# Keeping layer 0's residual in the PSUM bank of its aggregation (two graph layers, 16 graphs)

## The reference

```
def layernorm(x): m = mean(x, -1); v = var(x, -1); return (x - m) / sqrt(v + 1e-5)

# layer 0: scores between all pairs of nodes, masked by the adjacency
e0    = leaky(einsum('id,jd->ij', h * a0, h))         # slope 0.2
alpha = sigmoid(where(adj == 1, e0, -inf))
x     = layernorm(x + einsum('ij,jd->id', alpha, h) + bias)

# layer 1: attention from two projected vectors
Hh    = x @ W;  s = Hh @ a_src;  d = Hh @ a_dst
e     = where(adj != 0, exp(-leaky(s_i + d_j)), 0)
x     = layernorm(x + elu((e @ Hh) / rowsum(e)))
```

## Time and profile before

| | us |
|---|---|
| median of 3 runs | 1370.85 (1370.57 to 1371.18) |
| the profiled execution | 1369.6 |
| its span, first to last instruction | 1367.8 |

### The profile page before, as it was taken

The page is one execution under the profiler, slowest core; times in us unless marked ns, Lnnn a source line. Parts: engine busy times, 40 slices in busy tenths (PEclk is TensorE's granted clock), DMA queues, the critical chain, the costliest instruction groups (busy, mean ns, idle before and its releaser), DMA issues.

```text
span 1367.8 us, 27395 instructions
## 1 busy us (share of the span) xinstructions
PE 1275.9 (93%) x7874; PEld 1139.3 (83%) x7874; DVE 1029.2 (75%) x2594; ACT 856.0 (63%) x2130; POOL 842.4 (62%) x1228
## 2 busy tenths in 40 slices
PE   5799999999999999999999999999999998999986
PEld 4788888888888888888888888888888888888875
DVE  5777778787777877778777787877878777787865
ACT  4746757476575756757476575756757567574643
POOL 4746749476583855839466583865839567394732
PEclk9999999999999999999999999999999999999999
DMA  8162350614325162350624415153250623406001
GB/s 173 32 109 74 67 109 19 119 58 87 94 41 102 45 111 73 59 113 12 121 63 73 104 28 110 54 100 80 54 119 16 111 73 65 108 14 124 28 5 34
DMA packets 190352, 101.73 MB, mean 74 GB/s; under 512 B 140656, under 2 KB 173808, under 8 KB 190320
## 3 DMA queue, kind: packets, MB, share of 16 engines
q1 hardware_dynamic: 171888, 67.79, 21.2%
q0 software_dynamic: 18432, 33.56, 14.6%
HBM read 84.55 MB, written 16.78 MB: 74 GB/s over the span
## 4 chain that ended last, share of the span: by engine, by line
PE 39%; POOL 24%; DVE 20%; issue 11%; ACT 5%; DMA 0%; DVEq 0%; POOLq 0%; ACTq 0%
POOL coef_lo L369 13%; PE acc_bank L1227 11%; PE hh_bank L1206 5%; DVE coef L880 5%; PE acc_bank L1108 4%; PE acc_bank L1110 4%; PE acc_bank L1109 4%; PE lg_bank L1108 3%; PE lg_bank L1110 3%; PE lg_bank L1109 3%; POOL var_eps L377 3%; POOL rstd L380 2%; POOL rstd L390 2%; DVE stats L920 2%; DVE reluP L915 2%
## 5 line engine op out<-in xcount | busy, mean ns | idle before, releaser
L1227 PE MATMUL acc_bank<-H,coef 128*128 128x258 f32 x2048 | 469.1, 382 | 10.9 <-ACT reluP L606 9.6
L1227 PEld LDWEIGHTS acc_bank<-H,coef 128*128 128x128 f32 x2048 | 381.7, 190 | 73.7 <-issue 20.2
L369 POOL TENSOR_TENSOR coef_lo<-coef,coef_hi 128x1024 fp32r<-128x1024 f32 x128 | 305.7, 2389 | 62.2 <-ACT coef_hi L552 60.3
L1108 PE MATMUL acc_bank<-h_hi,coef_hi 128*128 128x256 f32 x1024 | 297.4, 290 | 0.0
L1110 PE MATMUL acc_bank<-h_hi,coef_lo 128*128 128x256 f32 x1024 | 286.3, 280 | 0.0
L1109 PE MATMUL acc_bank<-h_lo,coef_hi 128*128 128x256 f32 x1024 | 286.1, 279 | 0.0
L880 DVE SCALAR_TENSOR_TENSOR coef<-tr_bank,E_col,codeT 128x256 f32<-128x256 f32 x512 | 209.1, 476 | 39.3 <-PE acc_bank L1227 36.8
L1108 PEld LDWEIGHTS acc_bank<-h_hi,coef_hi 128*128 128x128 f32 x1024 | 194.8, 190 | 1.0
L1109 PEld LDWEIGHTS acc_bank<-h_lo,coef_hi 128*128 128x128 f32 x1024 | 195.0, 190 | 0.0
L1110 PEld LDWEIGHTS acc_bank<-h_hi,coef_lo 128*128 128x128 f32 x1024 | 194.7, 190 | 0.0
L552 ACT ACTIVATE coef_hi<-coef 128x1024 fp32r<-128x1024 f32 x128 | 135.7, 1060 | 84.6 <-DVE coef L819 84.1
(11 more groups left out here) (77 smaller groups left out, 2283.5 us busy)
## 6 DMA issues: line engine op xcount, KB each, us to landing
code_nat<-in_adj POOLq DMA_DIRECT2D x128, 256.0 KB, 5.3
x_raw<-in_x SPq DMA_DIRECT2D x16, 1024.0 KB, 5.6
out<-x SPq DMA_DIRECT2D x128, 128.0 KB, 1.7
codeT<-code_nat SPq DMA_TRANSPOSE x128, 3.3
W_ext<-in_L_gnn_W SPq DMA_DIRECT2D x1, 256.0 KB, 4.2
eluE<-in_L_gnn_a SPq DMA_DIRECT2D x1, 256.0 KB, 4.6
bias_bc<-in_L_gnn_bias SPq DMA_DIRECT2D x1, 128.0 KB, 4.1
a_col<-in_L_gnn_a SPq DMA_DIRECT2D x4, 1.0 KB, 4.6
```

The source lines that it names most:

```text
L369: nc.gpsimd.tensor_tensor(coef_lo[:, t % 4, :, :], blocks(coef[:, t % 4, :]), f32(coef_hi[:, t % 4, :, :]), ALU.subtract).then_inc(S.lo0, 1)
L1108: nc.tensor.matmul(dst, lhs_hi, rhs_hi, start=first, stop=False)
L1227: ins = nc.tensor.matmul(acc_bank[t % 2][:, 0:HC], coef[:, SLOT1[t], J * P:(J + 1) * P], H[:, J, :], start=J == 0, stop=J == NT - 1)
```

## The change

The SBUF tile `resid` goes. `residual0` writes its result over its own input, in columns 0 to 255 of the PSUM bank; `stats0` and `norm0` read it there. The bank is therefore free for the next matmuls only when `norm0` is done, so the two waits of PE that protected the bank change from the residual's semaphore to `x1`, with the same counts.

```
--- before.py
+++ after.py
@@ -192,7 +192,7 @@
         coef = sb("coef", [P, 6, N])
         coef_hi = sb("coef_hi", [P, 4, NT, P], FP32R)
         coef_lo = sb("coef_lo", [P, 4, NT, P], FP32R)
-        resid = sb("resid", [P, 2, D])
+
         stats = sb("stats", [P, 4, 6])
         moments = sb("moments", [P, 4, 2])
         var_eps = sb("var_eps", [P, 4, 1])
@@ -829,12 +829,12 @@
                 dve.wait_ge(S.agg0, NT * b + t + 1)
                 if t == 0:
                     dve.wait_ge(S.xb, NT * b + NT)
-                nc.vector.scalar_tensor_tensor(resid[:, t % 2, :], acc_bank[t % 2][:, 0:D], 0.5, xb[:, t, :],
+                nc.vector.scalar_tensor_tensor(acc_bank[t % 2][:, 0:D], acc_bank[t % 2][:, 0:D], 0.5, xb[:, t, :],
                                                ALU.mult, ALU.add).then_inc(S.resid0, 1)
 
             def stats0(S, b, t):
                 dve.wait_ge(S.resid0, NT * b + t + 1)
-                nc.vector.bn_stats(stats[:, t % 2, :], resid[:, t % 2, :]).then_inc(S.stats0, 1)
+                nc.vector.bn_stats(stats[:, t % 2, :], acc_bank[t % 2][:, 0:D]).then_inc(S.stats0, 1)
 
             def moments0(S, b, t):
                 dve.wait_ge(S.stats0, NT * b + t + 1)
@@ -846,7 +846,7 @@
                 if prev:
 
                     dve.wait_ge(S.out_stored[t], 16 * b)
-                nc.vector.tensor_scalar(x1[:, t, :], resid[:, t % 2, :], moments[:, t % 2, 0:1],
+                nc.vector.tensor_scalar(x1[:, t, :], acc_bank[t % 2][:, 0:D], moments[:, t % 2, 0:1],
                                         rstd[:, t % 2, :], ALU.subtract, ALU.mult).then_inc(S.x1, 1)
 
 
@@ -1167,7 +1167,7 @@
                     pe.wait_ge(S.h_lo, 4 * b + 4)
 
                 if t >= 2:
-                    pe.wait_ge(S.resid0, NT * b + t - 1)
+                    pe.wait_ge(S.x1, NT * b + t - 1)
                 elif prev:
                     pe.wait_ge(S.relu, NT * b + t - 1)
                 for J in range(NT):
@@ -1222,7 +1222,7 @@
                 if t >= 2:
                     pe.wait_ge(S.relu, NT * b + t - 1)
                 else:
-                    pe.wait_ge(S.resid0, NT * b + t + 7)
+                    pe.wait_ge(S.x1, NT * b + t + 7)
                 for J in range(NT):
                     ins = nc.tensor.matmul(acc_bank[t % 2][:, 0:HC], coef[:, SLOT1[t], J * P:(J + 1) * P],
                                            H[:, J, :], start=J == 0, stop=J == NT - 1)
```

## The result

The changed kernel takes 1398.75 us (median of 4 runs, 1395.96 to 1399.19) against 1370.71 for the kernel before (median of 4): the ratio is 1.0201, with a 95% interval of 1.0183 to 1.0218. It is 28 us slower; 20 were forecast, with a range that reached to 28. The profiled execution took 1395.96 us with a span of 1394.3.

The account below looks back on a forecast made before the run. Taken as bound: a closed loop without slack through PE, ACT, POOL and DVE. A 1.84 us delay less 0.27 at tiles 2 and 3 gives 1.30 per graph; 16 x 1.30 = 20.8 us on 1369.6, plus 1.25: 1391, range 1380 to 1399.

Parts of the forecast that it names:

- Only one new wait: In PE's order, only the aggregation of tile 2 gets a real new wait, for x1 of tile 0, 16 times.
- Its size: Aggregation of tile 2 on PE starts at 547.32 in place of 545.48, 1.84 us later.
- No cover on ACT and POOL: ACT's rounding of tile 5, POOL's low part and 1/sqrt of tile 2 all come 1.84 us later.
- The normalisation at 0.54: DVE's normalisation reading PSUM takes 0.54 us in all cases: 0.13 more where alone, 0.27 less where it met POOL.
- The residual and the statistics keep their size: On DVE, a PSUM source costs nothing that shows: residual 416 ns and statistics 425 ns keep their durations.
- The sum of +1.30 for one graph: x1 of tile 2 comes 1.57 us later, tile 3 1.30 later at PE; 16 graphs give 20.8 us.
- From there PE runs on, and the shift is kept to the end of the graph: After x1 of tile 3, from PE's 562.38, the +1.30 us shift stays to the graph's end.
- The low and high ends: Low 1381 from normalisation at 0.41 and POOL's small operations; high 1399 from 0.06 us on PSUM write and read.
- The rival on the faster side: PE's idle 1.57 us at tile 1 absorbs the wait, normalisation's gain stays: 8 us faster, 1363; chance 0.08.
- The rival of a dearer DVE: Each of three DVE operations on PSUM costs 0.2 us more: 1.9 per graph, 30 us, 1401; chance 0.11.

Follow-up runs that it names:

- the run that changed ACT's order: Changed kernel with ACT's rounding of tile 5's coefficients moved directly behind its copy of transposed tile 0, in step 2: 1382.41 us, ratio 1.0091.
- PE filled at both waits: Changed kernel plus unread matmuls, 3 ahead of the new wait and 4 ahead of the transpose of tile 2: 1387.05 us, ratio 1.0122.
- the run of the wait alone: Kernel before with only PE's two waits changed to x1; residual, statistics and normalisation stay in SBUF: 1404.93 us, ratio 1.0263.

## Why the prediction was right, and what it missed

- **Only one new wait:** right. It appears 16 times, ahead of tile 2, and the other changed waits nowhere.
- **Its size:** 1.85 us later against 1.84. PE shows it as idle time of 1.5 to 1.6 in most graphs, since it got to the wait a little later.
- **No cover on ACT and POOL:** right in the trace (3.43 and 2.73 us of idle time), and by the run that changed ACT's order.
- **The normalisation at 0.54:** right, 0.540. The sum of a PSUM source's 0.416 and 0.06 for each of two column operands came out at the right number; no run changes the column operands alone. The Trainium skill's cap ("VectorE: DVE Perf Modes", Why PSUM operands drop a tier) agrees with 0.54 against 0.41. The Trainium skill's rule that such an instruction doesn't contend with GpSimd ("SBUF — State Buffer", Who interferes with whom) agrees too: 0.546 at most with the additions beside it.
- **The residual and the statistics keep their size:** right within 9 ns. The 65 ns estimated from the Trainium skill's cycle table ("VectorE: DVE Perf Modes", The TRN2 errata) are not seen: 425 against 429 for the statistics when their source moved to PSUM.
- **The sum of +1.30 for one graph:** right at PE's transpose of tile 3, and 1.21 as the mean of the graphs without a stretch at the lower clock. With PE filled at both waits, the whole kernel is 16.8 us slower than before, against 20.8 forecast: this part was 4 us too high. (1391.65, the forecast's own sum, rounds to 1392, not 1391.)
- **What failed** is the sentence "From there PE runs on, and the shift is kept to the end of the graph". PE doesn't run on at the same speed: behind the wait of tile 2, which I had not sized (it grew from 0.66 to 2.09 us, as the idle time of tile 1 moved there), seven graphs have 3.4 us at half speed, 1.18 us each. That term was missing from the sum: 8 us in the profiled execution, whose granted clock was 0.989, and 11.7 by the medians with and without filling (the other three executions had 0.984 or 0.985). The low and high ends had been made for the costs on DVE and POOL alone, and the result lies at the range's upper end for this reason. That it lies inside, 0.25 us below 1399, is luck: the missing term and the 4 us too many of the delay partly cancel, and one of the four executions (1399.19) is outside.
- **The rival on the faster side** is out as it stood, since the wait isn't absorbed. The gain of about 0.5 us per graph that it counted on is there, but only where the wait is not (tile 0 in SBUF, 1360.64). The rival of a dearer DVE is out by the sizes and by the run of the wait alone.

## What to carry to other kernels

Writing a result back into the accumulator's bank prolongs the bank's occupation to its last reader; look in the order of the matrix engine for the one place where the next use of the bank comes before that reader is asked for anyhow, and keep that tile out. When an engine's idle time seems to cover a delay, follow also what other engines wait for from the delayed step. And when one large wait replaces several small ones on the matrix engine, allow for a stretch at half clock behind it, and look for a later wait that would take up the loss: here 3.4 us at half clock cost nothing where 0.66 and 0.56 us of waits followed, and 1.18 where 0.30 did.

## What the runs showed that I had not expected

Behind the empty 2.1 us at tile 2 the clock fell in seven of 16 graphs. Behind the new wait of 1.6 us it fell in none, but behind the wait of 1.59 us at tile 1 of the kernel before it fell in two, so the length of the wait alone doesn't settle it: neighbouring graphs with the same waits come out differently, at 83.91 and 85.09 us. Eight matmul instructions without any use, 1.89 us in that gap, made the kernel 10.7 us faster (1398.75 to 1388.02). And the changed kernel's one benefit, a normalisation that no longer meets POOL, was to be had more cheaply: moving eight additions on POOL gave 1359.64 us, the fastest of all that ran, within the spread of the version with tile 0 in SBUF.
